# First tiles turned inside the V products, K's low weight halves apart, a normaliser that works by head, and the first layer's tile ahead of the last pair's features

## What is computed

```python
xn = layernorm(x)
# two graph convolutions: D^-1/2 (A + I) D^-1/2 (h W^T) + b, with relu between
g = gcn(relu(gcn(xn, W1, b1)), W2, b2)
# linear attention, 12 heads of 64, 256 random features m
q, k, v = split(xn @ W_qkv)
phi = lambda t: exp(t @ features.T - 0.5 * sum(t * t)) / 16
kv, k_sum = phi(k).T @ v, sum(phi(k))
a = (phi(q) @ kv) / (phi(q) @ k_sum + 1e-6)
y = layernorm(xn + a @ W_proj + b_proj) * gamma + beta
x = x + g + y
# eight experts: of the router's two best per row the higher index is used
x = x + silu(layernorm(x) @ w1[e]) @ w2[e]
```

## Time and profile before

| what | value |
|---|---|
| median of 3 runs | 2406.55 us (2404.95 to 2407.1) |
| the profiled execution | 2406.96 us, span 2405.2 us |
| mean granted TensorE clock | 0.990 |
| TensorE busy | 2321.0 us (96%) |
| VectorE busy | 1257.5 us (52%) |
| ScalarE busy | 870.3 us (36%) |
| GpSimd busy | 846.9 us (35%) |
| chain that ended last | TensorE 82%, VectorE 8%, ScalarE 6%, issue 3%, DMA 1% |

### The profile page before, as it was taken

One profiled execution on the slowest core, in us unless ns is written; L12 is line 12 of the kernel. 1 busy time (PEld: TensorE's weight loads), 2 busy tenths in 40 slices (PEclk: granted clock), 3 DMA queues, 4 the chain that ended last, 5 costly groups with the idle time before them and its releaser, 6 DMA issues.

```text
span 2405.2 us, 43961 instructions
## 1 busy us (share of the span) xinstructions
PE 2321.0 (96%) x16441; PEld 1582.9 (66%) x16441; DVE 1257.5 (52%) x2846; ACT 870.3 (36%) x1330; POOL 846.9 (35%) x617
## 2 busy tenths in 40 slices
PE   5999999999999999999999999999999999999697
PEld 3878787878666666676666666666665666666475
DVE  6757575745767676765214344344341443444455
ACT  3546464635747474552113223223221000000075
POOL 1001216567677787776551111111100000000164
PEclk9999999999999999999999999999999999999889
DMA  7878886653331313224237767767755454443163
GB/s 281 290 282 282 272 279 161 178 139 73 66 67 1 66 0 66 24 30 111 48 55 238 236 202 221 224 203 219 226 175 209 120 192 155 177 147 148 54 202 129
DMA packets 166775, 375.87 MB, mean 156 GB/s; under 512 B 73950, under 2 KB 80968, under 8 KB 160748
## 3 DMA queue, kind: packets, MB, share of 16 engines
q1 hardware_dynamic: 90220, 313.83, 37.5%
q0 software_dynamic: 69216, 40.47, 13.6%
q10 hardware_dynamic: 7200, 19.69, 2.1%
HBM read 222.79 MB, written 156.63 MB: 158 GB/s over the span
## 4 chain that ended last, share of the span: by engine, by line
PE 82%; DVE 8%; ACT 6%; issue 3%; DMA 1%; SPq 0%; DVEq 0%; ACTq 0%; POOL 0%; POOLq 0%
PE pair L1933 33%; PE pair L397 31%; PE pair L1749 5%; PE pair L1729 3%; PE pair L1679 2%; DVE arena L1368 2%; DVE arena L1370 2%; DVE arena L1374 2%; ACT arena L961 2%; PE pair L2076 2%; PE pair L2089 1%; PE pair L1738 1%; ACT arena L887 1%; PE pair L1853 1%; ACT arena L971 1%
## 5 line engine op out<-in xcount | busy, mean ns | idle before, releaser
L397 PE MATMUL pair<-arena 128*128 128x384 f16 (+3 forms) x5760 | 891.2, 316 | 5.3 <-issue 3.4
L752 POOL DMA_INDIRECT cells<-arena x392 | 658.6, 1680 | 567.4 <-DMA cells<-arena 431.9
L1933 PE MATMUL pair<-arena 128*128 128x384 f16 x4900 | 813.4, 326 | 0.9 <-DVE arena L1544 0.9
L397 PEld LDWEIGHTS pair<-arena 128*128 128x128 f16 x5760 | 562.7, 98 | 316.5 <-issue 6.8
L1933 PEld LDWEIGHTS pair<-arena 128*128 128x128 f16 x4900 | 474.0, 98 | 306.5 <-issue 1.3
L788 POOL DMA_INDIRECT slots<-arena x25 | 24.4, 978 | 473.3 <-DVEq L1597 440.1
L1749 PE MATMUL pair<-arena 128*128 128x66 f32 x1200 | 155.8, 273 | 1.6 <-ACT arena L930 1.2
L1749 PEld LDWEIGHTS pair<-arena 128*128 128x128 f32 x1200 | 146.9, 193 | 4.3 <-ACT arena L930 1.5
L930 ACT ACTIVATE arena<-pair,arena 128x256 f32<-128x256 f32 x300 | 125.8, 478 | 65.6 <-PE pair L1729 64.9
L1034 ACT ACTIVATE arena<-arena 128x768 f32<-128x768 f32 x25 | 23.4, 935 | 334.5 <-DVE arena L1469 334.5
L1853 PE MATMUL pair<-arena 128*128 128x320 f32 (+1 forms) x480 | 131.2, 427 | 0.0
(11 more groups left out here) (207 smaller groups left out, 2436.4 us busy)
## 6 DMA issues: line engine op xcount, KB each, us to landing
cells<-arena SPq DMA_DIRECT2D x50, 800.0 KB, 9.7
ahl_dram<-arena SPq DMA_DIRECT2D x23, 1600.0 KB, 10.7
arena<-ahl_dram SPq DMA_DIRECT2D x23, 1600.0 KB, 6.8
arena<-in_x SPq DMA_DIRECT2D x70, 384.0 KB, 3.8
arena<-key_dram SPq DMA_DIRECT2D x28, 896.0 KB, 5.8
arena<-cells SPq DMA_DIRECT2D x25, 800.0 KB, 7.4
arena<-cells POOLq DMA_DIRECT2D x25, 800.0 KB, 7.6
split_w<-arena SPq DMA_DIRECT2D x32, 384.0 KB
```

The source lines that it names most:

```text
L397: ins = nc.tensor.matmul(dst[half], left(k, a), right(k, b, half), start=start and n == 0, stop=stop and n == 2)
L752: nc.gpsimd.indirect_dma_start(cells[k], bass.IndirectOffsetOnAxis(ap=idx_all[:, m:m + 1], axis=0), val_all[:, m:m + 1], None, bounds_chec ...
L1933: ins = nc.tensor.matmul(pair[u][:, half, 0:HD], a[:, 0, s * P:(s + 1) * P], X[part][:, s, half * HD:(half + 1) * HD], start=(s == 0 and p ...
```

## The change

- The weights are loaded in halves, V first, then K, and the random features behind them. ScalarE casts and VectorE subtracts halves of 768 columns.
- TensorE starts its V products as soon as tile 0 is turned; tiles 1 to 4 are turned inside the products of V tiles 0 to 3, at fixed blocks. Within V tile 0 each block waits for its own low weights. K's low halves are awaited before the first K product. ScalarE evicts V tiles 0 to 2 between the others' evictions.
- The tiles of chunk 0 and `krow` lie elsewhere, so `kv` and the columns of `vals` are cleared by GpSimd before its last signal `consts`.
- VectorE makes the row keys after tile 2's low half and the column keys after tile 4's; the random features' halves are split last. `key_made` is still signalled after the targets.
- `normaliser` and `normalise` keep each head's rows at that head's partitions, in one `den`. In pairs 0 to 4 VectorE does the first step for both heads, one second step over 128 rows, then the third step for each; in pair 5 it goes head by head. The square of head 1 (cast and subtraction) moves to the start of the pair that uses it.
- In the last pair of the last chunk `z1_rows(0, 0)` stands ahead of feature part 1.

```diff
-        x0 = [at(RX + 13542 + D * j, D) for j in range(TC)]
+        x0 = [at(RT + 9984 + D * j, D) for j in range(TC)]
         eint = [at(RX + 8880 + ET * i, ET, dt=I32) for i in range(8)]
-        krow, ktmp = at(RX + 1200, ET), at(RX + 1620, ET)
+        krow, ktmp = at(RT + 13824, ET), at(RT + 13824 + ET, ET)
...
-        den = [at(RX + 3760, CW), at(RX + 17502 + CW, CW)]
+        den = at(RX + 3760, CW)
...
+        def split_v_hi(act, m):
+            act.wait_ge(w_in_sem[m], 16)
+            nc.scalar.copy(kv_w(m, 0, 1), staged(m)[:, 1, :]).then_inc(w_hi_done, 1)
+
+        def split_v_lo(dve, m):
+            dve.wait_ge(w_hi_done, m + 1)
+            nc.vector.tensor_tensor(kv_w(m, 1, 1), staged(m)[:, 1, :], kv_w(m, 0, 1), ALU.subtract).then_inc(w_lo_done, 1)
+
+        def split_k_hi(act, m):
+            act.wait_ge(w_k_in, 16 * K)
+            nc.scalar.copy(kv_w(m, 0, 0), staged(m)[:, 0, :]).then_inc(w_hi_done, 1)
+
+        def split_k_lo(dve, m):
+            dve.wait_ge(w_hi_done, K + m + 1)
+            nc.vector.tensor_tensor(kv_w(m, 1, 0), staged(m)[:, 0, :], kv_w(m, 0, 0), ALU.subtract).then_inc(w_k_lo, 1)
...
+            def load_weights(m, v, done):
+                sp.dma_start(staged(m)[:, v, :], kv_src(m)[:, v * D:(v + 1) * D]).then_inc(done, 16)
...
             for m in range(K):
-                load_weights(m)
+                load_weights(m, 1, w_in_sem[m])
+            for m in range(K):
+                load_weights(m, 0, w_k_in)
+            for h in range(2):
+                sp.dma_start(rf[h * DH:(h + 1) * DH, :], rf_t).then_inc(consts_in, 16)
...
+            made.link(nc.gpsimd.memset(kv, 0.0))
+            made.link(nc.gpsimd.memset(vals[:, :, :, DH:VW], 0.0))
...
+            split_v_hi(act, 0)
             root(0)
+            split_v_hi(act, 1)
             for n in range(TC):
                 high(n)
-                split_hi(act, n, n + 1)
+                if n == 0:
+                    split_v_hi(act, 2)
+                if n == 1:
+                    split_v_hi(act, 4)
+                    split_v_hi(act, 5)
+                if n >= 2:
+                    split_k_hi(act, 2 * (n - 2))
+                    split_k_hi(act, 2 * (n - 2) + 1)
+                    if n == 2:
+                        act.wait_ge(consts, 2)
+                    evict_v(0, n - 2)
                 evict_hi(n)
+                if n == 0:
+                    split_v_hi(act, 3)
...
-                rows = ln_den[(1 - h) * DH:(2 - h) * DH]
                 if h == 0 and (not isinstance(m, int) or m):
                     act.wait_ge(a_ready, 2 * m)
-                nc.scalar.activation(halves_of(rows, c), bank_pair(1 + s, c)[DH:P],
+                nc.scalar.activation(halves_of(ln_den[rows], c), bank_pair(1 + s, c)[DH:P],
                                      ACT.Ln, bias=eps6[DH:P, 0:1]).then_inc(den_ready, 1)
                 act.wait_ge(den_ready, 4 * m + 2 * h + 1)
-                n = 2 * half_cols(c)
-                nc.scalar.activation(den[h][DH:P, 0:n], rows[:, 0:n], ACT.Exp, scale=-1.0).then_inc(den_ready, 1)
+                nc.scalar.activation(den[rows, 0:n], ln_den[rows, 0:n], ACT.Exp, scale=-1.0).then_inc(den_ready, 1)
...
                     features(c, p, 0)
+                    square_high(c, p, 1)
...
-                    if next_up:
-                        square_high(*nxt, 1)
...
+            for n in range(TC):
+                if n < K // 2:
+                    split_v_lo(dve, 2 * n)
+                    split_v_lo(dve, 2 * n + 1)
+                low(n)
+                if n == TC - 2:
+                    normal(n + 1)
+                if n >= TC - 2:
+                    split_k_lo(dve, 2 * (n - TC + 2))
+                    split_k_lo(dve, 2 * (n - TC + 2) + 1)
+                if n >= LO_ACT:
+                    dve.wait_ge(x_tr_lo, n + 1)
+                    nc.vector.tensor_copy(xT_tile(n, 1), halves6(bank16(6))).then_inc(ev_lo, 1)
+                if n == TC - 1:
+                    edge_keys(4, kcol)
+                    split_k_lo(dve, 4)
+                    split_k_lo(dve, 5)
+                    edge_targets(eint[5], eint[7], eint[6])
+                    dve.sem_inc(key_made, 1)
+                if n < TC - 2:
+                    normal(n + 1)
+                if n == TC - 3:
+                    dve.wait_ge(consts, 2)
+                    dve.wait_ge(edges_in, 64)
+                    edge_keys(0, krow)
+            split_features()
...
+            def normalise(c, p, one_by_one):
+                m, n = c * PAIRS + p, 2 * half_cols(c)
+                head = [slice(h * DH, (h + 1) * DH) for h in range(2)]
+                cn = Chain(dve, dve_done, c * (q_links + y_links) + (q_base + 3 * p))
+
+                def first_step(h):
+                    s = q_use[("o", p, h)][0]
+                    dve.wait_ge(den_ready, 4 * m + 2 * h + 2)
+                    cn.link(nc.vector.scalar_tensor_tensor(halves_of(ln_den[head[h]], c), bank_pair(1 + s, c)[DH:P], 1e-6,
+                                                           halves_of(den[head[h]], c), ALU.add, ALU.mult))
+
+                def second_step(rows):
+                    cn.link(nc.vector.scalar_tensor_tensor(den[rows, 0:n], ln_den[rows, 0:n], 2.0, den[rows, 0:n],
+                                                           ALU.subtract, ALU.mult))
+
+                def third_step(h):
+                    s = q_use[("o", p, h)][0]
+                    if h == 0 and (not isinstance(m, int) or m):
+                        dve.wait_ge(a_lo, m)
+                    nc.vector.scalar_tensor_tensor(halves_of(a_f[head[h]], c), bank_pair(1 + s, c)[0:DH], -1.0,
+                                                   halves_of(den[head[h]], c), ALU.mult, ALU.mult).then_inc(a_ready, 1)
+                    dve.wait_ge(a_ready, 2 * m + h + 1)
+                    dve.sem_inc(qp_free[s], 1)
+
+                if one_by_one:
+                    for h in range(2):
+                        first_step(h)
+                        second_step(head[h])
+                        third_step(h)
+                else:
+                    first_step(0)
+                    first_step(1)
+                    second_step(slice(0, P))
+                    third_step(0)
+                    third_step(1)
...
+                    square_low(c, p, 1)
...
-                    normalise(c, p, 0)
-                    if next_up:
-                        square_low(*nxt, 1)
-                    normalise(c, p, 1)
+                    normalise(c, p, p + 1 == PAIRS)
...
+            turn_first_hi(0)
+            turn_first_lo(0)
+            first_hi = {(0, 2): 1, (1, 2): 2, (2, 1): 3, (2, 5): 4}
+            first_lo = {(0, 4): 1, (1, 4): 2, (2, 3): 3, (3, 1): 4}
...
-            pe.wait_ge(w_lo_done, K)
...
+                        if c == 0:
+                            pe.wait_ge(w_k_lo, K)
+                            pe.wait_ge(ev_hi, TC)
+                            pe.wait_ge(ev_lo, TC)
...
+                        if c == 0 and t == 0:
+                            pe.wait_ge(w_lo_done, k + 1)
+                        if c == 0 and (t, k) in first_hi:
+                            turn_first_hi(first_hi[t, k])
+                        if c == 0 and (t, k) in first_lo:
+                            turn_first_lo(first_lo[t, k])
...
-                    q_features(c, p, 1)
                     if not more and p == PAIRS - 1:
                         pe.wait_ge(g1_in, 16 * T + 16 * K)
                         pe.wait_ge(q_copied, UNITS)
                         z1_rows(0, 0)
+                    q_features(c, p, 1)
```

127 lines of the change are left out of this document (44 added, 83 removed).

## The result

The changed kernel took 2394.24 us (median), the kernel before 2406.7 on the same chip: the ratio is 0.9946, 95% interval 0.9933 to 0.9959. So it is faster by 12.5 us where 16.3 were forecast, inside the range.

The account below looks back on a forecast made before the run. TensorE works almost without pause, so gains must come from its pauses: 2.6 + 12.1 + 1.6 = 16.3 us off 2406.96 gives 2390.7, with the median 0.4 lower 2390.3, rounded 2390; range 2386 to 2395.

Parts of the forecast that it names:

- Part 1: First stage: first tiles turned inside V products, with half copies, casts and subtractions; 2.6 us gained, bounds 0.5 to 6.
- pause: Before the first norms: of 11.3 us that TensorE wins at the start, 6.9 are pause again.
- Rival (e): First products: turns and waits hold the level at 1.2 GHz throughout, so the kernel is slower, 2416 us; chance 0.02.
- the clock rose: First products: the clock rises 3.3 us after the product's start, which costs 1.7 us.
- Part 2: Attention stage: normaliser by head, ending TensorE's pause in the pairs; 12.1 us gained, bounds 5 to 14.5.
- the ring: Attention pairs at 640 columns: ScalarE and VectorE's cycle shortens from 13.12 to 12.52 us, against TensorE's 12.47.
- rival d: Attention: the 128-row step's 0.86 is wrong by 0.6, so only part 1 pays; 2402 to 2404 us, chance 0.07.
- head 1's first step 1.46 after head 0's: VectorE's normaliser in attention: gap between the heads' first steps, 1.46 us of the 4.15 that replace 5.25.
- rival (a): Attention: the ring stays longer than TensorE's work, 12.8 instead of 12.5; 7 us lost, 2397 us, chance 0.15.
- Part 3: Last attention pair: the first layer's tile stands ahead of the wait for a bank; 1.6 us gained.
- In at about 8.4 us behind the last q product: First layer's tile: its six weight copies, issued at 1083.64, land at about 1092 and the tile can start then.
- Rival (b): Layer 1's entry: GpSimd's chain ends no earlier, or later; 2392 us at best, 2395 with a slip of 3; chance 0.07.

Follow-up runs that it names:

- e5: Changed kernel plus VectorE's first-pair low keys after three of chunk 1's five statistics and ScalarE's chunk-1 root behind the last V tile: 2391.24 us, ratio 0.9934.
- e11: Changed kernel plus edits of e6, e9, e8, chunk 1's root behind the first norms' copy, first pair's second square made earlier; slower chip: 2400.32 us, ratio 0.9892.
- e1: The whole changed kernel as it is, run again for a profile at its usual pace: 2391.99 us, ratio 0.9943 to the kernel before.
- e9: Changed kernel with the square of the q rows made on VectorE instead of ScalarE; third, slower chip: 2410.55 us, ratio 0.9934.
- e7: Changed kernel with TensorE taking both weight products of feature parts 2 and 3 ahead of their norm products: 2393.3 us, ratio 0.9945.
- e4: Kernel before with only the first layer's tile moved ahead of feature part 1 of the last pair: 2406.32 us, ratio 0.9997.
- e6: The kernel of e5 with pair 1's low keys also made ahead of pair 0's one-hot marks on VectorE: 2391.74 us, ratio 0.9938.
- e10: The whole changed kernel once more, unaltered, on the third, slower chip: 2412.84 us, ratio 0.9947 to the kernel before.
- e3: Kernel before with only the normaliser's part (five VectorE steps a pair, head 1's square moved to the next pair's start): 2398.86 us, ratio 0.9978.
- e8: Changed kernel with layer 1's first tile starting on three of its six weight tiles, its second half waiting for the others: 2392.82 us, ratio 0.9945.
- e2: Kernel before with only the start's part (weight halves, turns inside V products, clears on GpSimd, order of edge keys): 2403.22 us, ratio 0.9989.

## Why the prediction was right, and where it was not

**Part 1** was followed almost to the half microsecond. Product start 18.3 (18.29), last low turn 41.1 (41.07), K's wait 1.3 (1.15), pause 6.9 (6.43), norms 65.4 (64.92), clock 1.8 (2.5), net 2.6 (2.3). Beyond K's wait the moved edge keys, K subtractions and clears show no cost, as said. e5 and e11 show by experiment what the pause hangs on: the late tile of x, in two places, VectorE's low keys and ScalarE's root. With both out of its way the pause is gone and the level holds at this place (1.00 from 58 to 71 us in e11). Whether it is then kept is not shown: the one profiled execution has a low stretch at 74.1.

**The pace of the first products.** Rival (e) didn't come about. Weight loads are 0.32 us apart up to 21.77 and about 0.16 behind 22.09 (timeline of the weight loads), so the full pace comes 3.5 to 3.8 us after the product's start at 18.29, with the first group of turns just there (L1739). Before, read the same way, it was 3.1 to 3.5. All later groups of turns take 0.50 as in the earlier trace rows.

```profile
21.45 0.15 PEld L405 LDWEIGHTS pair<-arena 128*128 128x128 f16 x1 [0.17 <-issue]
21.77 0.15 PEld L1739 LDWEIGHTS pair<-arena 128*128 128x128 f16 x1 [0.17 <-issue]
...
22.43 1.62 PEld L405 LDWEIGHTS pair<-arena 128*128 128x128 f16 x11
```

The prediction says that "the clock rose" there. The granted clock doesn't show it: it is 1.00 from 18.3 to 21.7 us in e1 and from 33.8 to 37.3 in the kernel before, so the slow start is seen in the distances alone, and its cause stays open. The Trainium skill (TensorE: Matmul & The Clock Gate, Part 4: PE-mode transpose) says that the full clock doesn't engage for transposes, which don't count as busy time in the same way; at this share, six turns to 12 wider matmuls, the trace shows no harm from them.

**Part 2: the mechanism was right, the ring was mis-sized by 0.11 us.** The waits on the bank went from 24 to none in mid-stage, the 128-row step costs 0.82 (rival d falls). But the term "head 1's first step 1.46 after head 0's" measures 964.63 - 963.05 = 1.58. I had let head 1's logarithm begin where the cast had begun, at 963.72, which is 0.64 behind the start of head 0's exponential (963.08). A logarithm in the same place starts 0.76 behind it (962.28 to 963.04 in e1, the same in every pair looked at), and the 0.12 between the two is the error. The ring was so 12.63 instead of 12.52, above TensorE's 12.47 by 0.16 and not 0.05, and what I called "the pause goes" left 0.16 us a pair, worth 3.6 us over the stage (e9). It is rival (a) at about half its price (0.16 a pair for 0.3, 3.6 us for 7). In the first pair the moved square cost 1.1, as forecast (1.11 in the waits); the lead fell by 1.5 there in all. From 5.9 to 16.1, the rest of the stage made 10.2 us, where 13.2 were forecast. e7 and e9 tell the causes apart: moving TensorE's need didn't help, taking 0.74 us off ScalarE did.

**Part 3: the landing was mis-sized, and the level was left out.** "In at about 8.4 us behind the last q product" measures 9.9 in e1 (issue at 1067.59, tile at 1077.45), and 9.0 to 9.6 in e4, e5, e6, e7, e9 and e10. When the level holds, 0.6 to 1.1 us are won at the tile instead of 1.6 (e4, e5, e6, e9 and e10, each against the trace before). In e1 and e7 a low stretch followed the wait, which I had weighed for the start and not here, and 1.2 and 1.0 us were lost. The wait's length alone doesn't tell which: 2.62 and 2.20 us were followed by the fall, 2.84 (e9), 2.00 (e10) and the 2.55 of the kernel before were not. Against part 2 without it, part 3 pays 2.4 in e1 (e3), and with the weights in halves 2.7 to 4.2 more (e11 against e10, e8 against e1).

**After attention** nothing caught up: GpSimd's chain and ScalarE's counts (1250.05) came in time, and the lead at layer 1 is the lead at the end. Rival (b) falls.

**The sum.** 16.3 forecast, 15.0 in the pair of traces, 12.5 to 13.7 by the medians. In the traces the terms are 2.3 + 10.2 - 1.5 (first pair) - 1.2, about 10, and 5 more, of which 4.5 are low stretches that this execution happened not to have. So the trace's nearness to the forecast is in part luck. The medians are the fairer figure, but their agreement isn't earned in full either: the forecast is too high by the 3.6 of the ring and, in e1, the 2.8 of the last pair, 6.4 in all, and the medians are only 2.6 to 3.8 below it. The terms read from e1 leave 2.7 to 3.9 us of the median gain without an explanation, about 2 less if the level usually holds at the tile. How many low stretches a typical execution of each kernel has stays open: only mean clocks exist for the others, 0.990 or 0.991 for 22 of the 26 executions before on e1's chip, and 0.988 to 0.990 for the whole change there.

## What to carry to other kernels

When a change shortens a ring that runs across two engines, add up the new ring start by start, with the measured distance of the very pair of instructions that will now be neighbours. Here 0.12 us a pair, of the 0.16 by which the ring outlasts TensorE, lay in one such distance: a cast had started 0.64 us behind an exponential, the logarithm that took its place started 0.76 behind it. And a TensorE wait can cost more than its length when a low stretch follows it (2.5 us at the norms and 1.4 at the tile in e1); so look at every place where the changed kernel will still wait, give the low stretch a chance of its own there, and remove all instructions that hang on the same late transfer together. Of two such instructions e5 removed one and kept 2.9 us at the 350th matmul of its trace, e11 both and kept 6.2 against e10 at the 500th.

## What the runs showed of the hardware that was not expected

Under steady TensorE work the granted clock falls to 0.5 for stretches of 3.4 us, not at the same places in two executions of one kernel (531 us in e10, not in e1). Five whose cost could be read took 1.2 to 1.7 us each. They aren't spread evenly: eight of the twelve traces at the usual pace (before and e1 to e11) have at least one between 526 and 599 us. They are a likely source of the spread between executions, since e8's lie 7.6 us apart with mean clocks from 0.990 down to 0.988, but only one execution of each run was profiled.

Behind waits of TensorE the traces show this. Between the first product and 2240 us there are nine waits of 3.0 to 6.6 us, eight of them in front of the first norms or the K product behind them and one at the last pair (e3), and each came with a low stretch of 3.4 or 6.8 us. Of six waits of 2.0 to 2.9 us at the first layer's tile or at the last pair's bank, two were followed by one (2.62 in e1, 2.20 in e7) and four were not (2.55 in before and in e2, 2.84 in e9, 2.00 in e10). What decides between them no run tells.

And one chip ran both the kernel before and the changed one 0.8 to 0.9% slower (2425.79 against 2405.7 and 2406.15, 2412.84 against 2391.99), while the ratios stayed; in the traces of the changed kernel 14 us of the difference lie behind 2197 us.
